# Spectral mix of a Fourier layer on TensorE: four 32x32 weight blocks, tiled apart or on the diagonal of one 128x128 stationary operand

## What is computed

```python
for sw, cw, cb in (...four layers...):
    x_ft = jnp.fft.rfft2(x, norm='ortho')                    # x: (B, 32, 64, 64)
    out  = jnp.einsum('bixy,ioxy->boxy', x_ft[:, :, :20, :20], sw)   # 32x32 weights for each of 20x20 modes
    x1   = jnp.fft.irfft2(out, s=(64, 64), norm='ortho')
    x    = gelu(x1 + jnp.einsum('bchw,oc->bohw', x, cw) + cb)
```

## Time and profile before

| what | value |
|---|---|
| timed runs | 8647.60, 8664.17, 8669.62 us; median 8664.17 |
| span of the profiled execution | 12469.6 us |
| instructions in the profile | 153,471; of them 25,600 matmuls and 25,600 weight loads of L417 |
| busy share of the span | PE 52%, PEld 38%, DVE 40%, ACT 27%, POOL 48% |
| HBM traffic | 461 MB read, 37 GB/s |

### The profile page before, as it was taken

How to read it: one execution, slowest core, us unless ns; L and a number is a source line. 1 busy time by engine, 2 the same in 40 slices (tenths; PEclk the granted TensorE clock), 3 DMA queues, 4 the chain that set the end, 5 groups by cost and what they waited for, 6 DMA issues and landing times.

```text
span 12469.6 us, 153471 instructions
## 1 busy us (share of the span) xinstructions
PE 6502.1 (52%) x51536; PEld 4676.4 (38%) x51536; DVE 5016.0 (40%) x16213; ACT 3311.9 (27%) x9871; POOL 5950.0 (48%) x6157
## 2 busy tenths in 40 slices
PE   7845364555645566464654645555565555424203
PEld 6633243442534434343343433444344433213102
DVE  2253524435253443525345253452524435352612
ACT  2212222223222232222322222222322223222222
POOL 0024545445454554545455454454545445565573
PEclk7755555556555565555555555555555555555555
DMA  1011111111111111111111111111111111111110
GB/s 29 12 28 39 44 38 43 37 38 40 35 42 39 41 39 37 45 35 41 36 40 42 35 41 39 39 41 36 38 40 42 38 36 41 39 42 39 41 49 25
DMA packets 251313, 474.14 MB, mean 38 GB/s; under 512 B 130470, under 2 KB 130974, under 8 KB 250143
## 3 DMA queue, kind: packets, MB, share of 16 engines
q0 software_dynamic: 196608, 403.05, 12.2%
q1 hardware_dynamic: 53856, 60.52, 1.7%
HBM read 461.04 MB, written 2.10 MB: 37 GB/s over the span
## 4 chain that ended last, share of the span: by engine, by line
issue 30%; PE 29%; DVE 17%; another core or an unknown queue 16%; DVEq 5%; ACT 3%; DMA 0%; SPq 0%; ACTq 0%; POOL 0%; POOLq 0%
PE MM L417 3%; DVE KV L849 3%; PE PB L1107 3%; PE PB L1080 2%; ACT GATH L842 2%; PE PB L1145 2%; DVEq L823 2%; PE PB L1104 2%; PE PB L1121 2%; PE PB L1135 1%; PE MM L371 1%; DVE I L786 1%; DVE PF L824 1%; PE MM L432 1%
## 5 line engine op out<-in xcount | busy, mean ns | idle before, releaser
L624 POOL DMA_INDIRECT GATH<-in_table,IDX x6144 | 5946.4, 968 | 6393.3 <-DVE KV L849 3878.1
L842 ACT ACTIVATE GATH<-GATH,WT 128x128 f32<-128x128 f32 x6144 | 1902.5, 392 | 198.0 <-issue 197.1
L849 DVE TENSOR_REDUCE KV<-GATH 128x128 f32<-128x2048 f32 x384 | 1390.7, 3622 | 679.4 <-ACT GATH L842 407.6
L417 PE MATMUL MM<-SPEC,SW 32*32 32x8 f32 x25600 | 613.6, 196 | 1688.7 <-issue 1646.1
L417 PEld LDWEIGHTS MM<-SPEC,SW 32*32 32x32 f32 x25600 | 519.8, 147 | 1800.0 <-issue 1792.4
L485 ACT ACTIVATE U<-MM 128x320 f32<-128x320 f32 (+1 forms) x416 | 219.5, 528 | 1853.3 <-remote 879.6
L526 DVE COPY TURN<-TP 80x512 f32<-80x512 f32 (+1 forms) x512 | 347.2, 685 | 890.1 <-remote 440.0
L485 ACT ACTIVATE SPEC<-MM 128x160 f32<-128x160 f32 x320 | 96.1, 301 | 2238.0 <-PE MM L417 1423.5
L371 PE MATMUL MM<-F,TURN 128*128 128x80 f32 x2048 | 422.9, 375 | 442.0 <-DVE TURN L526 350.6
L371 PEld LDWEIGHTS MM<-F,TURN 128*128 128x128 f32 x2048 | 391.8, 284 | 506.0 <-issue 266.4
L456 PEld LDWEIGHTS MM<-G,TURN 80*128 80x128 f32 x2048 | 344.9, 241 | 522.7 <-issue 243.8
(11 more groups left out here) (201 smaller groups left out, 11175.6 us busy)
## 6 DMA issues: line engine op xcount, KB each, us to landing
GATH<-in_table,IDX POOLq DMA_INDIRECT x6144
SW<-in_sw SPq DMA_DIRECT2D x160, 320.0 KB
CONV<-in_cwb SPq DMA_DIRECT2D x128, 4.0 KB
CONV<-in_cwb SPq DMA_DIRECT2D x128, 0.1 KB
U<-in_xT SPq DMA_DIRECT2D x16, 96.0 KB
out<-OUTB SPq DMA_DIRECT2D x16, 96.0 KB
W1E<-in_w SPq DMA_DIRECT2D x1, 520.0 KB
W2E<-in_w SPq DMA_DIRECT2D x1, 512.0 KB
```

Source lines behind the costliest of these rows:

```text
L417: m = e.matmul(pv[r, :, k, :], SW[r, c % 2, k, :], Sv[r, :, c * MODES + k, :], start=True, stop=True)
L624: e.indirect_dma_start(GATH[:, r, k, :], None, table, bass.IndirectOffsetOnAxis(IDX[:, u // H, u % H, k:k + 1], 0)).then_inc(gath[r], 16)
L842: m = e.activation(GATH[:, r, k, :], GATH[:, r, k, :], ACT.Copy, scale=WT[:, u // H, u % H, k:k + 1])
L849: e.tensor_reduce(KV[:, u // H, u % H, :], GATH[:, u % RING, :, :].rearrange("p k d -> p d k"), AX.X, ALU.add).then_inc(S["gather_free"], 1)
```

## The change

`SW` becomes two half-chunk buffers of 10 modes, each mode a 128x128 matrix: zero but for the four 32x32 blocks on its diagonal. One matmul with all 128 rows then does what four did: 20 matmuls a chunk. The buffer is zeroed once at the start, and each half is loaded by four DMAs (one block of partitions each, runs of 128 bytes in SBUF). Half 0 of the next chunk waits for a new semaphore, raised when TensorE has used half 0 of this one; half 1 waits for the end of the chunk. The buffer grows from 5 KB to 10 KB a partition. A rename of loop variables at L794 changes nothing that runs.

```diff
+HALVES, HM = 2 * CHUNKS, MODES // 2
...
-        SW = sb("SW", [128, 2, MODES, WID])
+        SW = sb("SW", [128, 2, HM, 128])
...
-        def sp_chunk(e, l, c):
-            e.dma_start(SW[:, c % 2, :, :].rearrange("p m o -> p (m o)"), sw[bass.ds((l * CHUNKS + c) * 128, 128), :]).then_inc(sw_in[c % 2], 16)
+        def sp_half(e, l, n):
+            for a in range(Q4):
+                e.dma_start(SW[32 * a:32 * a + 32, n % 2, :, 32 * a:32 * a + 32],
+                            sw[bass.ds((l * CHUNKS + n // 2) * 128 + 32 * a, 32), HM * WID * (n % 2):HM * WID * (n % 2 + 1)].rearrange("i (m o) -> i m o", o=WID)).then_inc(sw_in[n % 2], 16)
...
             e.wait_ge(mm_full, CREDIT + mm_layer(g, l))
-            sp_chunk(e, l, 0)
-            sp_chunk(e, l, 1)
+            sp_half(e, l, 0)
+            sp_half(e, l, 1)
...
         def sp_mix(e, g, l):
-            for c in range(2, CHUNKS):
+            for c in range(1, CHUNKS):
                 yield c - 0.8
-
-                e.wait_ge(mm_full, CREDIT + mm_layer(g, l) + GB * F_T + c - 1)
-                sp_chunk(e, l, c)
+                e.wait_ge(sw_used, (g * LAYERS + l) * CHUNKS + c)
+                sp_half(e, l, 2 * c)
+                yield c - 0.4
+                e.wait_ge(mm_full, CREDIT + mm_layer(g, l) + GB * F_T + c)
+                sp_half(e, l, 2 * c + 1)
...
             for c in range(CHUNKS):
                 yield c
-                per_layer = (CHUNKS + 1 - c % 2) // 2
-                e.wait_ge(sw_in[c % 2], 16 * (per_layer * (g * LAYERS + l) + c // 2 + 1))
                 p = mm_slot(e, mb, c)
-                fence(e)
                 pv = p[:, 0:Q4 * GB * MODES * 2].rearrange("p (q m r) -> p q m r", q=Q4 * GB, r=2)
-                for k in range(MODES):
-                    for a in range(Q4):
-                        r = slice(32 * a, 32 * a + 32)
-                        m = e.matmul(pv[r, :, k, :], SW[r, c % 2, k, :], Sv[r, :, c * MODES + k, :], start=True, stop=True)
-                m.then_inc(mm_full, 1)
+                for half in range(2):
+                    e.wait_ge(sw_in[half], 16 * Q4 * (CHUNKS * (g * LAYERS + l) + c + 1))
+                    fence(e)
+                    for k in range(HM):
+                        at = HM * half + k
+                        m = e.matmul(pv[:, :, at, :], SW[:, half, k, :], Sv[:, :, c * MODES + at, :], start=True, stop=True)
+                    m.then_inc(mm_full if half else sw_used, 1)
...
-                for t in (FW0, FW1, FW2, CONV, KB, ONES, RS, OHS, AREA4):
+                for t in (FW0, FW1, FW2, CONV, KB, ONES, RS, OHS, AREA4, SW):
                     e.memset(t[:], 1.0 if t is ONES else 0.0).then_inc(zeroed, 1)
```

## The result

The changed kernel takes 8,876.8 us (median of four runs, 8,850.6 to 8,900.0); the kernel before, run beside it, 8,656.1 us (four runs, 8,647.6 to 8,669.6). The ratio is 1.026, 95% interval 1.0235 to 1.0284: slower by 221 us, where I forecast 151. The profiled execution took 8,900.03 us, so this time the trace is one of the timed runs; it is the slowest of the four, 23 us above their median.

The account below looks back on a forecast made before the run. TensorE was taken to bound the kernel before 665 us, POOL's gathers at 480 us a round afterwards. First group 72, first window 24, rounds 52 and start 2 sum to +150 on 8,664: 8,815 us, range 8,640 to 9,120.

Parts of the forecast that it names:

- The budget of POOL: GpSimd's gathers: 6,144 at 1.25 us plus both ends give 8,471 of 8,664 us, leaving 193 us of waits.
- A chunk is 40 x 206 = 8.2 us at the half clock: New mix on TensorE: 40 pairs a chunk at 206 ns each, so a layer's mix takes 41 us, not 23.
- The first group's term of +72: Four layer mixes before the first gather: 4 x 41 - 92 = +72 us, all exposed.
- the start's +2: Zeroing SW at the start, where SyncE was already waiting: 2.3 us, counted as +2.
- First window of round -1, +24: Window before the gathers, where TensorE is the bound: the dearer mix adds 24 us, exposed.
- The rounds, 13 x 4 = +52: 13 rounds with layers and gathers: windows of 228 and 252 us sum to POOL's 480; +4 us a round.
- if the overshoot shows: Case for the rounds: first window's 228 us against 220 of gathers shows, costing 8 us a round instead of 4.
- The rival of the windows in series: Rounds: TensorE-bound first and VectorE-bound second windows add without slack, 13 x 24 = 312 us instead of 52; 9,075 us; chance 0.20.
- The half load, 3.2 us, hidden by 0.9: Loading half 0 of the next chunk takes 3.2 us, hidden behind half 1's 4.1 us of multiplying at half clock.
- Full clock: Rival: continuous weight loads hold TensorE's clock at 1.0, chunks take 4.4 us; about 8,665 us; chance 0.10.
- Late weights: Rival: a half load takes 6 us and TensorE waits 1.9 at each half; about 9,175 us; chance 0.13.
- Starved TensorE: Rival: timed runs partly have TensorE's "issue" stalls beside gathers, which a quarter of the instructions frees; 8,610 us; chance 0.15.

Follow-up runs that it names:

- e2: The changed kernel with each layer's weights loaded for its first chunk only and used by all five: 12,611.8 us, ratio 0.9945 to the kernel before on the same chip.

## Why the prediction was right or wrong

**The budget of POOL.** Right in what it was for, and it carried the forecast: profiled rounds of some 730 us didn't fit in 8,664. Of the cause I said nothing; it is the pace of the run, not the profiler. But the 193 us aren't all waits. I took each gather at 1.25 us where the page's mean of 968 ns makes 1.268; in the kernel after this and other small gaps are 136 us. If they are as much in the kernel before, it waits some 75 us in all, not 193 (8,654 - 665 - 7,680 - 98 - 136), with no 12 a round. Had I summed against the span of 12,469.6, its single matmuls would have argued for a gain, and at that pace rightly so for the part beside gathers.

**A chunk is 40 x 206 = 8.2 us at the half clock.** Right: 8.53 to 8.68 us from the second chunk on, 213 ns a pair. One reason for the half clock was misread: the new mix moves a quarter of the old one's columns (40 x 8 against 160 x 8), not a third. The first group's term of +72 came out at +79, the start's +2 at +2 or less.

**First window of round -1, +24.** The term itself holds: 22 to 24 us between windows of equal clock. The window grew by 46 because its clock was 0.58 instead of 0.66. I had no term for that; 22 of the 70 missing us are here. Two kernels show the same swing between executions of unchanged instructions; whether the change makes the lower clock more likely is open.

**The rounds, 13 x 4 = +52.** Mis-sized, and this is the step that failed most: about +97 after the first gather at the median, 119 in the traced run. I put the windows at 228 and 252, sum 480, just POOL's own. They measure 263.5 and 231.9, or 243 and 255: the first is longer, in part by its clock (0.58, 0.59), the second under my 252 or near it (VectorE 209 to 211 us busy), and the sums are 495 and 498. POOL's own pace is 487, though, and in rounds 1 to 12 it waits 114.1 us for the ring, 9 a round. That is the 8 which I had set for the case "if the overshoot shows", where I took 4. The rival of the windows in series would be 312 us in the rounds and isn't borne out: most of what TensorE has more to do in a round stays hidden. I also had no term for round 0, where POOL waits 80.5 us until the ring's first units are used. How much of the loss behind the first gather is round 0's, and how much is the matmuls', the clock's or the loads', is open: no trace of the kernel before and no experiment exists at this pace.

**The half load, 3.2 us, hidden by 0.9.** Right: 3.0 us from first issue to last data in the kernel after and some 0.4 more until TensorE can use them, hidden by about 0.7, although the old load has twice the bytes of a half, not four times as the rival put it. When one issue of the four is slow it shows, in waits of 0.3 to 0.6 us in the first group; nine of them in the whole trace come to 5.9 us. e2 shows that the loads cost nothing before the first gather. What 410,000 small packets cost in the rounds is shown at the slower pace only, about 94 us.

**The rivals.** Full clock: no, 0.53 in the mix. Late weights: no at the timed pace; at the other TensorE does wait for them (478 us, up to 32.7), but in the wait of 31 us that I followed the load was issued late and wasn't slow itself. Starved TensorE: the changed kernel isn't at the timed pace, where the mix's weight loads wait 41.8 us for "issue" in all. How far the kernel before is, no trace shows; whatever the three quarters of the mix's instructions freed there, it was less than the change cost. At the other pace the wider matmuls give 184 us back, not enough against 122 for the start and 94 for the loads. The profile alone didn't contain at which of the two paces a run would go; the timed median did.

## What to carry to other kernels

Merging small tiled matmuls into one padded stationary removes instructions, not time, once instructions are at hand: four 32x32 tiles abreast took 2.3 us a chunk, two 64x64 ones 4.4, one of 128x128 8.7. Before such a merge, ask whether TensorE waits for instructions in the timed runs, and take a span that is far above the median as a reason to look at what in it can't be true of them. Where the windows of a round sum to just the pace of the engine that leads, what is put into one of them is exposed in part: here each window got a mix some 20 us dearer, by the durations ahead of the gathers, and POOL waited 9 us a round. And before taking an engine's pace from its shortest row, compare it with the mean on the page: 0.95 us against 0.968 is 110 us over 6,144 gathers.

## What the runs showed of the hardware that I had not expected

- Two paces: the kernel before takes 8,656 us in one place and 12,470 to 12,674 on four other chips. A gather costs the same to issue (965 to 969 ns) and its packets have moved 1.2 us later at both. At the slower one TensorE, ScalarE and VectorE each idle 1,419 to 1,619 us for "issue" beside the gathers in the changed kernel, against 4 to 30 at the faster.
- The granted clock of one window differs between executions of one kernel, 0.58 or 0.65, worth 23 us of 227, with the start of the window 0.3 us apart: one execution has the full clock for 27.3 us where the other has the half. A stretch bound by TensorE carries that uncertainty.
- Four DMAs of 40 KB in 128-byte runs have moved 3.0 us after the first issue when the four issues take 1.9 us, about as long as the old load of twice the bytes, 3.3 us. Where one of the four issues takes a microsecond or more, TensorE waits for them even behind a half of 4.3 us.
